# A sparse-attention kernel on one core: GpSimd's late moves ahead of adjacency loads and conversions, two of eight conversions of the adjacency on VectorE, the accumulator's base loaded one step earlier

## The reference

```python
h = jnp.maximum(_layernorm(x, axis=-1), 0.0)
adj = jnp.maximum(adjacency_matrix, eye)
q, k, v = (jnp.einsum('nd,hdk->hnk', h, W) for W in (Wqs, Wks, Wvs))
scores = jnp.einsum('hqk,hmk->hqm', q, k) * kd ** (-0.5)
scores = scores + IDENTITY_BIAS * eye - MASK_VAL * (1.0 - adj)
att = jax.nn.softmax(scores, axis=-1)
x = x + jnp.einsum('hqm,hmk,hko->qo', att, v, Wo)
```

## Time and profile before

| what | value |
|---|---|
| median of 3 runs | 2718.37 us (2713.33 to 2725.66) |
| profiled execution | 2709.6 us, span 2708.1 us, mean granted clock 0.994 |
| TensorE busy | 2630.7 us, 97% of the span |
| VectorE, ScalarE busy | 2253.6 us (83%), 1850.8 us (68%) |
| GpSimd busy | 1280.6 us (47%), of it 1007.8 us late moves (line 307) |
| share of the chain that ended last | TensorE 38%, SyncE's queue 3%, VectorE 2%, DMA 2% |

### The profile page before, as it was taken

The page is one execution under the profiler, slowest core; times in us unless marked ns, Lnnn a source line. Parts: engine busy times, 40 slices in busy tenths (PEclk is TensorE's granted clock), DMA queues, the critical chain, the costliest instruction groups (busy, mean ns, idle before and its releaser), DMA issues. The chain is left out here.

```text
span 2708.1 us, 58752 instructions
## 1 busy us (share of the span) xinstructions
PE 2630.7 (97%) x17344; PEld 1901.9 (70%) x17344; DVE 2253.6 (83%) x3833; ACT 1850.8 (68%) x3041; POOL 1280.6 (47%) x2418
## 2 busy tenths in 40 slices
PE   7899999999999999999998999999999999999997
PEld 5666777767777776766766777777777777777775
DVE  6788888888888888888847888888888888888885
ACT  3576777767767676776745777777777777777774
POOL 2356655566565556655512444444444444343433
PEclk9999999999999999999999999999999999999999
DMA  6367766677776677776652566656565656555654
GB/s 163 111 143 177 184 163 175 165 168 167 173 190 170 164 177 166 171 171 169 167 142 76 146 158 151 158 142 145 138 151 145 164 146 162 133 146 138 157 144 106
DMA packets 263358, 418.51 MB, mean 155 GB/s; under 512 B 98944, under 2 KB 119936, under 8 KB 259200
## 3 DMA queue, kind: packets, MB, share of 16 engines
q1 hardware_dynamic: 172032, 228.88, 33.0%
q0 software_dynamic: 89088, 184.69, 29.7%
q10 hardware_dynamic: 2176, 4.19, 0.4%
HBM read 136.31 MB, written 46.27 MB: 67 GB/s over the span
## 5 line engine op out<-in xcount | busy, mean ns | idle before, releaser
L307 POOL DMA_DIRECT2D S<-S x2048 | 1007.8, 500 | 1137.1 <-DVE S L723 1089.6
L702 DVE CUSTOM_DVE_ANT_0 S<-psS,B 128x1024 f32<-128x1024 f32 x1024 | 1228.4, 1218 | 268.3 <-PE psS L449 155.1
L589 ACT ACTIVATE S<-S,negm 128x1024 f32<-128x1024 f32 (+1 forms) x768 | 1095.8, 1428 | 88.8 <-DVE negm L709 88.3
L596 ACT ACTIVATE PT<-psT 128x512 f32<-128x512 f32 x1024 | 595.0, 596 | 267.5 <-PE psT L462 248.5
L449 PE MATMUL psS<-K,QH 128*128 128x512 f32 x2048 | 729.2, 437 | 35.7 <-DVE mx L702 31.5
L449 PE MATMUL psS<-K,QL 128*128 128x512 f32 x2048 | 642.5, 395 | 0.0
L462 PEld LDWEIGHTS psT<-ident,S 128*128 128x128 f32 x4096 | 481.2, 140 | 192.0 <-issue 73.5
L462 PE MATMUL psT<-ident,S 128*128 128x128 f32 x4096 | 608.0, 276 | 7.8 <-ACT S L589 4.9
L723 DVE STREAM_TRANSPOSE S<-S 128x2048 f32<-128x2048 f32 x256 | 590.2, 2306 | 27.6 <-PE psO L486 23.7
L472 PE MATMUL psO<-PT,V 128*64 128x256 f32 x4096 | 492.1, 382 | 0.0
L486 PE MATMUL psO<-S,V 128*64 128x256 f32 x4096 | 470.3, 382 | 2.0 <-DMA S<-S 2.0
(11 more groups left out here) (51 smaller groups left out, 967.9 us busy)
## 6 DMA issues: line engine op xcount, KB each, us to landing
S<-S SPq DMA_DIRECT2D x2048, 64.0 KB, 3.1
S<-S POOLq DMA_DIRECT2D x2048, 64.0 KB, 2.9
B<-in_adj POOLq DMA_DIRECT2D x128, 256.0 KB, 7.2
bias_scratch<-B SPq DMA_DIRECT2D x32, 1024.0 KB, 5.8
B<-bias_scratch SPq DMA_DIRECT2D x128, 256.0 KB, 5.1
hq<-hT_scratch SPq DMA_DIRECT2D x32, 256.0 KB, 3.5
RB<-rden_scratch SPq DMA_DIRECT2D x128, 64.0 KB, 3.2
S<-in_x SPq DMA_DIRECT2D x8, 512.0 KB, 3.6
```

Source lines behind the costliest of these rows:

```text
L307: pool.dma_start(dst, src).then_inc(late_sent[q][half], 16)
L589: nc.scalar.activation(part, part, ACT.Exp, bias=negm[:, h % 2, q:q + 1], accum_out=sums[:, h % 2, q, e:e + 1]).then_inc(probs_ready, 1)
L596: nc.scalar.activation(PT[:, s % RING, :], psT[s % 2][:, :], ACT.Copy).then_inc(pt_act, 1)
L702: nc.vector.tensor_tensor_reduce(out=part, in0=psS[j % 2][:, :], in1=B[:, q, k * SLOT:(k + 1) * SLOT], scale=SCALE, scalar=LOWEST, op0=ALU ...
```

## The change

1. In GpSimd's step 2, both row tiles' late moves come first, and then all four adjacency loads of row tile 0; before, two of the loads stood between the two late moves. In step 3, two conversions of row tile 1 that ended step 2 now stand between the two late moves.
2. Of a block's eight slots GpSimd converts six (`TAKEN`). Slots 6 and 7 are converted by VectorE just before their masks (`REST`); GpSimd's `add_self` only treats the own entries there while they are still 0 and 1 (zero through `notI`, then plus a new tile `eye`), in those blocks where they lie in slot 6 or 7, and signals `self_added`.
3. `load_base` stands behind `store` in step 1, and a semaphore `res_free` takes over what the order guaranteed, that `res` isn't overwritten before it is stored.

The diff, cut to its core:

```diff
 TS = (MT - LATE) // 2
 QUAD = P // 32
 HALVES = 2
+REST = 2
+TAKEN = SLOTS - REST
 SP_MOVES = [[((j - d) % QUAD, j) for j in range(2 * half, 2 * half + 2) for d in (1, 3)] for half in range(HALVES)]
 POOL_MOVES = [[((j - d) % QUAD, j) for j in range(2 * half, 2 * half + 2) for d in (0, 2)] for half in range(HALVES)]
 MOVED = 16 * len(SP_MOVES[0])
...
     late_sent = [[sem(f"late_sent{g}{q}{half}") for half in range(HALVES)] for q in range(QT)]
     adj_in = [[sem(f"adj_in{g}{q}{k}") for k in range(SPT)] for q in range(QT)]
     bias_kept = sem(f"bias_kept{g}")
+    res_free = sem(f"res_free{g}")
+    self_added, bias_rest = sem(f"self_added{g}"), sem(f"bias_rest{g}")
     (bias_conv, bias_ready, q_proj, q_hi, q_lo, scores_ready, slot_masked, row_ready, probs_ready,
      transposed, pt_act, pt_free, o_ready, projected, summed, den_ready, head_added,
      late_transposed, late_used, odd_copied, o_summed, rden_stored, rden_in) = (
...
 
         def keep_bias(i):
 
-            sp.wait_ge(bias_ready, i * SLOTS + SLOTS)
+            sp.wait_ge(bias_ready, i * TAKEN + TAKEN)
+            sp.wait_ge(bias_rest, i * REST + REST)
             for q in range(QT):
                 sp.dma_start(bias[bass.ds(i * QW + q * P, P), :], B[:, q, :]).then_inc(bias_kept, 16)
 
...
                 done = nc.gpsimd.tensor_tensor(own, own, notI[:, :], ALU.mult)
             done.then_inc(bias_ready, 1)
 
+        def add_self(i, own_slot):
+
+            if own_slot < SPT - REST:
+                pool.sem_inc(self_added, 1)
+                return
+            q = QT - 1
+            wait_apart(pool, adj_in[q][own_slot], i * 16 + 16, pool_passed)
+            own = B[:, q, bass.ds(i * QW + q * P, P)]
+            nc.gpsimd.tensor_tensor(own, own, notI[:, :], ALU.mult).then_inc(bias_conv, 1)
+            wait_apart(pool, bias_conv, i * QT + q + 1, pool_passed)
+            nc.gpsimd.tensor_tensor(own, own, eye[:, :], ALU.add).then_inc(self_added, 1)
+
         def move_late(i, h, q):
 
             wait_apart(pool, late_transposed, count(i, h, QT, q + 1), pool_passed)
...
+        pool.sem_inc(res_free, START)
         if norm:
             constants()
             pool.wait_ge(half_set, 1)
...
             with pool.Fori(1, NC // 2) as i:
                 for b in range(2):
                     inverse_deviation(i, b)
-            for q in range(QT):
-                for k in range(SPT):
-                    convert(0, q, k, 0)
+            for j in range(TAKEN):
+                convert(0, j // SPT, j % SPT, 0)
+            add_self(0, 0)
         load_base(0)
 
         def step(i, h, more, prev, own_slot):
             adj_step, adj_rest = more and norm and h == GROUP - 2, more and norm and h == GROUP - 1
             move_late(i, h, 0)
-            if adj_step:
-                for k in range(2):
-                    load_adj(i + 1, 0, k)
+            if adj_rest:
+                for k in range(SPT - REST):
+                    convert(i + 1, 1, k, own_slot)
             move_late(i, h, 1)
-            if adj_step:
-                for k in range(2, SPT):
-                    load_adj(i + 1, 0, k)
+            if adj_rest:
+                add_self(i + 1, own_slot)
             if prev and h == 1:
                 store(i - 1)
+                load_base(i)
             if prev and h == 2:
                 pool.wait_ge(stored, i * 16)
-                load_base(i)
+                pool.sem_inc(res_free, 1)
             if adj_step:
+                for k in range(SPT):
+                    load_adj(i + 1, 0, k)
                 for half_ in range(2):
                     for k in (2 * half_, 2 * half_ + 1):
                         convert(i + 1, 0, k, own_slot)
                     for k in (2 * half_, 2 * half_ + 1):
                         load_adj(i + 1, 1, k)
-                for k in range(2):
-                    convert(i + 1, 1, k, own_slot)
-            if adj_rest:
-                for k in range(2, SPT):
-                    convert(i + 1, 1, k, own_slot)
 
         for h in range(GROUP):
             step(0, h, True, False, 0)
...
         def mask(i, h, j, first=False):
 
             q, k = divmod(j, SPT)
-            if h == 0 and norm:
-                dve.wait_ge(bias_ready, i * SLOTS + (j + 1))
+            if h == 0 and norm and j < TAKEN:
+                dve.wait_ge(bias_ready, i * TAKEN + (j + 1))
+            if h == 0 and norm and j >= TAKEN:
+                dve.wait_ge(self_added, i + 1)
+                wait_apart(dve, adj_in[q][k], i * 16 + 16, dve_passed)
+                part = B[:, q, k * SLOT:(k + 1) * SLOT]
+                nc.vector.tensor_scalar(part, part, -1.0, MASK_VAL / SCALE, ALU.add, ALU.mult).then_inc(bias_rest, 1)
+                dve.wait_ge(bias_rest, i * REST + (j + 1 - TAKEN))
             if h == 0 and not norm:
                 dve.wait_ge(adj_in[q][k], i * 16 + 16)
             if not first and j >= SPT:
...
                 dve.wait_ge(base_in, i * 16 + 16)
             else:
                 dve.wait_ge(head_added, count(i, h, 1, START - 1))
+            if h == GROUP - 1:
+                dve.wait_ge(res_free, i + START)
             dst = res if h == GROUP - 1 else acc
             nc.vector.tensor_tensor(dst[:, :, :], psP[:, :].rearrange("p (q d) -> p q d", q=QT), acc[:, :, :],
                                     ALU.add).then_inc(head_added, 2)
...
         dve.sem_inc(o_summed, START)
         dve.sem_inc(o_ready, START)
         if norm:
-            dve.wait_ge(consts, 3)
+            dve.wait_ge(consts, 4)
             for b in range(2):
                 dve.wait_ge(h_out[b], 16 * (NC // 2 + START))
         for j in range(SLOTS):
```

More of the change, by code:

```diff
@@ L82, in group_programs @@
 def group_programs(nc, sem, g, before, x, hT, adj, bias, Wk, Wq, Wv, Wo, base, result, t):
-    (K2, V, S, B, PT, QH, QL, hq, wq, wo, O, Oodd, RB, acc, res, ident, notI, diag, mx, negm, sums, den, rden,
+    (K2, V, S, B, PT, QH, QL, hq, wq, wo, O, Oodd, RB, acc, res, ident, notI, eye, diag, mx, negm, sums, den, rden,
      stats, mv, rstd, half, xb, hc, wk, wv, psS, psT, psO, psP, rden_scratch, ones_set, consts) = t
@@ L324, in constants @@
             nc.gpsimd.memset(notI[:, :], 1.0).then_inc(ones_set, 1)
+            nc.gpsimd.memset(eye[:, :], 0.0).then_inc(ones_set, 1)
             nc.gpsimd.memset(diag[:, :], 0.0).then_inc(ones_set, 1)
-            pool.wait_ge(ones_set, 3)
-            for m, fill in ((ident, 1.0), (notI, 0.0), (diag, IDENTITY_BIAS)):
+            pool.wait_ge(ones_set, 4)
+            for m, fill in ((ident, 1.0), (notI, 0.0), (eye, 1.0), (diag, IDENTITY_BIAS)):
                 nc.gpsimd.affine_select(out=m[:, :], in_=m[:, :], compare_op=ALU.not_equal, fill=fill, base=0,
                                         pattern=[[-1, P]], channel_multiplier=1).then_inc(consts, 1)
-            pool.wait_ge(consts, 3)
+            pool.wait_ge(consts, 4)
+        pool.sem_inc(res_free, START)
         if norm:
@@ L531, in tensor_program @@
         if norm:
-            pe.wait_ge(consts, 3)
+            pe.wait_ge(consts, 4)
             transpose_x(0, 0)
@@ L843, in build @@
         notI = sb("notI", [P, P], BF16)
+        eye = sb("eye", [P, P], BF16)
         diag = sb("diag", [P, P])
@@ L865, in build @@
         ones_set, consts = sem("ones_set"), sem("consts")
-        tiles = (K2, V, S, B, PT, QH, QL, hq, wq, wo, O, Oodd, RB, acc, res, ident, notI, diag, mx, negm, sums, den, rden,
+        tiles = (K2, V, S, B, PT, QH, QL, hq, wq, wo, O, Oodd, RB, acc, res, ident, notI, eye, diag, mx, negm, sums, den, rden,
                  stats, mv, rstd, half, xb, hc, wk, wv, psS, psT, psO, psP, rden_scratch, ones_set, consts)
```

## The result

| kernel | median us | ratio to before, 95% interval |
|---|---|---|
| before | 2719.78 (2713.33 to 2725.66) | 1 |
| changed | 2742.12 (2739.72 to 2744.40) | 1.0087 [1.0068, 1.0106] |

What follows compares the result with a forecast made beforehand. TensorE was taken as the bound, with first-group waits for late moves blamed on GpSimd's order and full DMA engines. 15 x (-1.23 + 0.8) = -6.4, +1.4 gave -5 us: 2713 on the median, range 2691 to 2740.

Steps and rivals of the forecast that it cites:

- Stretch 3, -1.23 a block: Third stretch of a first-group block: late moves meet no load before theirs, so it falls to 20.15 us, -1.23 a block.
- The first load goes out at 10.6: GpSimd in stretch 3: second late move starts at 6.6, its 3.96 us end at 10.6, then the first load goes out.
- Mask 5 needs 22 engine-us from there: DMA work before stretch 4's mask 5: 16 for eight loads, 2.1 leftover moves, 4.1 for half of stretch 4's moves.
- At a share of 1.05 that is 21 us.: DMA engines from first load's data to mask 5: 22 engine-us take 21 us, putting mask 5 near 13.0 into stretch 4.
- Conversions at 0.7 each: VectorE before masks 6 and 7: each conversion 0.6 us plus 0.1 wait on its own result (0.5 to 1.35).
- Row tile 1's moves start near 10.5 and land before mask 7 at 18: GpSimd in stretch 4: these moves, behind two conversions, are all issued at 14.5; with add_self, nothing or 0.3 us at most.
- From mask 7 to the end 2.40: End of stretch 4: 2.40 us from mask 7, as today, within a new stretch of 20.2 against 19.4.
- Start +1.4: Block 0 before the loop: VectorE is the bound over masks 0 to 7, so both conversions show once, +1.4 us.
- Second group 0 to -1: Second group of heads: nothing else changes there, 0 to -1 us.
- C: Rival, chance 0.13: the loads' tail idles GpSimd and delays late moves; mask 5 at 14.5, +17 us, time 2736.
- A: Rival, chance 0.29: GpSimd's order, not the DMA engines, is the limit; mask 5 at 12.4, gain 14 to 20, time 2701.
- B: Rival, chance 0.14: VectorE converts one element a cycle, 1.35 us each; 19.5 us above the forecast, time 2733.

Runs made afterwards that it cites:

- half_before: The kernel before with adjacency loads of half the columns from block 1 on and a factor of 1 in the conversions: block 78.04 us, one execution.
- second pair of traces: The kernel before and the changed kernel, both unchanged, run and traced again on one chip: ratio 1.0090, blocks 79.73 and 81.64 us.
- no_vector: The changed kernel without VectorE's conversions, GpSimd doing all eight: ratio to before 1.0025.
- vector_early: The changed kernel with VectorE's conversions of slots 6 and 7 in front of masks 4 and 5: ratio to before 1.0028.
- loads_apart: The changed kernel with GpSimd's first two adjacency loads back between the late moves of step 2: ratio to before 1.0027.
- only_between: The kernel before with only the first two conversions of row tile 1 moved between the late moves of step 3: ratio 1.0032.
- loads_apart_again: The changed kernel with the first two loads back between step 2's late moves, run again on another chip: ratio to before 1.0054.
- after_again: The changed kernel, unchanged, run again on one chip with the kernel before: ratio to before 1.0090.
- keep_early: The kernel before with SyncE's write of B moved from the end of step 0 to right behind its late moves: ratio 0.9972.
- only_loads: The kernel before with all four loads of row tile 0 behind both late moves of step 2, nothing else: ratio 1.0146.

## Why the prediction was wrong

1. *Stretch 3, -1.23 a block.* Right: 21.52 to 20.27, with masks 6 and 7 at 15.61 and 16.94 (before 16.51 and 19.01). That the loads' bytes and not only GpSimd's order made it late is shown by half_before.
2. *The first load goes out at 10.6.* Right: 10.9.
3. *Mask 5 needs 22 engine-us from there.* Too low: 23.8 in the mean over 14 blocks (21.6 to 24.8), 23.0 in the shown one.
4. *"At a share of 1.05 that is 21 us."* This step failed, with the 22 that it divides. Mask 5 starts at 15.5 instead of 13.0. The way from the first load to mask 5, in the block shown of each kernel, before and then changed:

```profile
627.57:656.00 28.43, 27.71 (x183) 20.05 (x182) 22.33 (x42) 20.06 (x33) 23.84 (x42) 1.00 0.99 202
```

```profile
639.78:664.33 24.55, 23.06 (x159) 16.50 (x158) 19.70 (x33) 18.44 (x30) 19.32 (x32) 1.00 0.94 177
```

Neither order has 1.05 over this way. That is the share of the full windows alone, and the earlier trace rows has a window of 0.62 between them. With a start of 1.0 us and 0.5 to land, the forecast gave the way 22.5 us for 22 engine-us, a share of 0.98, which is the mean of the kernel before. The changed kernel has 0.96 in the mean of 14 blocks (0.93 to 0.99): GpSimd first waits 3.2 us (mean) for data with only late moves to fill the engines, and then sends loads in pairs. The holes of 0.86 and 0.71 are there. The way took 24.8 us for 23.8 engine-us. Of the 2.5 us that mask 5 was off, about 0.6 is the lower share, 1.7 the engine-us above 22, and 0.3 the later first load. Part of the 1.7 is that the same transfers kept the engines busy longer: 35.4 engine-us in stretches 3 and 4, against 33.6 before and 33.2 in the forecast (34.4 against 33.6 in the second pair of traces). Why they did is open. In time, stretch 4 rose by 3.2 us where 0.8 was forecast: 15 x 2.4 = 36 us. The spans differ by +30.0 where -5 was forecast, a miss of 35; what else was off, in 8, nearly cancels.
5. *Conversions at 0.7 each.* Right: 666.57 to 667.27 is 0.70; 0.42 us the conversion and 0.28 the wait for it. The two parts, 0.6 and 0.1, were each off and cancel in the sum. The estimate by the Trainium skill's table (VectorE: DVE Perf Modes, The perf-mode tier table) was 0.43, and the trace agrees with 421 ns.
6. *Row tile 1's moves start near 10.5 and land before mask 7 at 18.* They start at 10.9, but GpSimd's last quarter lands at 19.2 in the mean; mask 7 lost 0.1 by it in the mean (1.94 behind mask 6, forecast 1.84) and 1.15 in the shown block.
7. *From mask 7 to the end 2.40.* Right: 2.42.
8. *Start +1.4*: +0.3, less than the starts of two traces of one kernel differ by (118.8 and 118.2 us for before). *Second group 0 to -1*: it won 0.34 us a block, 5 us in all. All kernels with whole loads say the same: with the early base load (both changed, no_vector, vector_early, both loads_apart) the second group's block is 77.15 to 77.38 us, without it 77.46 to 77.88. *Stretch 2* wasn't in the sum: it rose from 18.90 to 19.24, another 5 us. The base load went there, but it doesn't explain it: stretch 2 is 18.83 in no_vector, which has it too. In the second pair of traces it is 18.94 and 19.01, so most of the 5 us is how much executions differ.

Of the rivals, C named the mechanism: the first conversion waits idle, the last loads go out near 3 us into stretch 4 (3.0 in the shown block), late moves right behind them. Its price was bounded at mask 5 = 14.5, and it came to 15.5; by its own rule, 15 us for each us of mask 5, that makes 17 + 15 = 32 us, and the spans differ by 30.0. Its chance of 0.13 was argued down with "those loads are few". That mask 5 after 14 would mean C was among the prediction's signs of being wrong, and it did. A is refuted as GpSimd's order being the limit: only_between sends the moves 3.2 us earlier and gains 0.55 at mask 5. Nor do SyncE's moves run unhindered by turns between queues, as A drew from the Trainium skill (DMA: Bandwidth & Descriptors, Queues, rings and completion order): those of row tile 0 in stretch 4 of the changed kernel take 6.6 us to land (median), against 2.9. B is refuted by 421 ns. That only the loads' place costs, or only VectorE's conversions, fell too: 1.0025 remains without the conversions, 1.0054 without the moved loads, 1.0087 to 1.0090 with both.

What is shown: the two loads' place puts mask 5 from 13.0 to 15.05 with all else equal on one chip (loads_apart_again, after_again), and VectorE's conversions cost 1.4 us of stretch 4 where they stand. What stays open: how the 2.1 us that the moved loads cost in stretch 4 divide between the holes in the DMA share, the transfers' longer time on the engines and SyncE's later start.

## What to carry to other kernels

Work for a shared resource is not only an amount: when its start is moved, draw up who issues the next piece and when, since the share that it had in the old order is not that of the new one. A transfer moved out of the way of one deadline should be followed to the next one; here 1.5 us won in one stretch cost 2.1 in the next. A share of a busy resource is averaged over the whole way that a sum covers, holes included. A short operation that moves to the busiest engine costs its duration and its wait if it stands in a chain that others wait for, and nearly nothing where that engine waits anyway: try the place before giving up the move.

## What the runs showed of the hardware

- The 1 KB store of the reciprocals takes 2.9 us to land in a stretch without loads (median), and 6.4 in stretch 3 of before, where GpSimd's loads are under way from another queue. With half the bytes in those loads it is 3.7. In the changed kernel it is 7.2 (up to 9.3) in one trace and 5.7 in the other, and behind the write of B, in stretch 1 of keep_early, 5.7. So a tiny transfer waits with the large ones around it, and what waits for it, SyncE's late moves, starts 0.6 to 1.4 us later in the changed kernel.
- In only_loads TensorE sits idle 3.67 us in the block shown, and the granted clock behind it is 0.50 in 673:676, where a pair of matmuls takes 1.22 us instead of 0.71. In each of 14 blocks there is such a drop.
- A conversion of 128 x 1024 in bf16 is 421 ns on VectorE and 1057 ns on GpSimd (mean of 96); 128 x 256 in f32 with two scalars from SBUF is 406 on VectorE.
- The kernel before has medians of 2703.0, 2704.0, 2704.2, 2719.8 and 2728.8 in five sets of runs, four of which were on four different chips: up to 1% apart. A ratio moved with the chip too (0.990 and 0.997 for one kernel on two chips).
